# P x V of a causal attention on one core: column halves of the array given to the two heads of a pair, and the scaling done on the way out of PSUM

## The reference, cut to what matters

```python
B, S, D = x.shape                      # 2, 1024, 1024 ; H = 32 heads
q = (_rmsnorm(x @ wq_a.T, q_a_ln_w) @ wq_b.T).reshape(B, S, H, QHD)
...
scores = jnp.einsum('bqhd,bkhd->bhqk', q_full, k_full) * softmax_scale
scores = jnp.where(causal[None, None], scores, jnp.finfo(scores.dtype).min)
attn = jax.nn.softmax(scores, axis=-1)
out = jnp.einsum('bhqk,bkhd->bqhd', attn, v).reshape(B, S, H * VD)
return out @ wo.T
```

## Time and profile before

| | us |
|---|---|
| runs of the kernel | 1892.49 median, 1891.0 to 1895.84 (3 runs) |
| span of the profiled execution | 1895.1 |
| PE busy in it | 1803.7 (95%) |
| DVE, ACT, POOL busy | 1231.4 (65%), 1000.5 (53%), 877.8 (46%) |
| one pass of the loop (two steps) | 60.5, 14 times |

### The profile page before, as it was taken

One profiled execution on the slowest core, in us unless ns is written; L12 is line 12 of the kernel. 1 busy time (PEld: TensorE's weight loads), 2 busy tenths in 40 slices (PEclk: granted clock), 3 DMA queues, 4 the chain that ended last, 5 costly groups with the idle time before them and its releaser, 6 DMA issues. The chain is left out here.

```text
span 1895.1 us, 44298 instructions
## 1 busy us (share of the span) xinstructions
PE 1803.7 (95%) x15472; PEld 1422.9 (75%) x15472; DVE 1231.4 (65%) x2654; ACT 1000.5 (53%) x2137; POOL 877.8 (46%) x641
## 2 busy tenths in 40 slices
PE   5999969899999999999999999998999999989999
PEld 4788869877777777777777777775788888877887
DVE  5655358688898888889888888989521111125453
ACT  2221047788887888888787888877310100112110
POOL 3232112377777878777787878775000000014321
PEclk9999979999999999999999999999999999989999
DMA  6542162311212112121222212123742233224321
GB/s 217 193 156 100 67 173 94 84 62 44 86 59 78 57 62 80 57 80 40 85 69 68 69 51 82 55 86 113 249 151 89 94 100 115 67 87 158 130 89 59
DMA packets 111969, 182.74 MB, mean 96 GB/s; under 512 B 27680, under 2 KB 64672, under 8 KB 109856
## 3 DMA queue, kind: packets, MB, share of 16 engines
q1 hardware_dynamic: 111904, 181.88, 29.8%
HBM read 122.33 MB, written 59.51 MB: 96 GB/s over the span
## 5 line engine op out<-in xcount | busy, mean ns | idle before, releaser
L1290 PE MATMUL psS<-keyT,q 128*128 128x512 f32 (+2 forms) x2304 | 473.2, 350 | 23.9 <-POOL q L648 14.5
L1290 PEld LDWEIGHTS psS<-keyT,q 128*128 128x128 f32 x2304 | 381.2, 189 | 118.2 <-DVE negmax L1408 41.7
L1357 ACT ACTIVATE prob<-prob,negmax 128x640 f32<-128x640 f32 (+7 forms) x512 | 392.0, 767 | 78.5 <-DVE negmax L1408 75.9
L1418 DVE STREAM_TRANSPOSE pT<-prob 128x640 f32<-128x640 f32 (+7 forms) x512 | 379.9, 762 | 66.4 <-PE psV L1307 61.6
L1408 DVE CUSTOM_DVE_ANT_0 prob<-psS,mask 128x640 f32<-128x640 f32 (+7 forms) x512 | 371.9, 742 | 20.9 <-PE psS L1290 7.4
L469 PE MATMUL f_psy<-f_weff,f_xT 128*128 128x512 f32 x1344 | 315.6, 393 | 0.0
L1101 PE MATMUL psS<-o_w,o_o 128*128 128x512 f32 x1344 | 304.8, 389 | 0.0
L469 PEld LDWEIGHTS f_psy<-f_weff,f_xT 128*128 128x128 f32 x1344 | 250.9, 188 | 55.8
L1101 PEld LDWEIGHTS psS<-o_w,o_o 128*128 128x128 f32 x1344 | 252.3, 188 | 52.4
L1307 PE MATMUL psV<-pT,val 32*64 32x512 f32 (+3 forms) x8192 | 264.8, 407 | 6.4 <-DVE pT L1418 6.2
L1307 PEld LDWEIGHTS psV<-pT,val 32*64 32x64 f32 x8192 | 168.8, 132 | 109.7 <-issue 66.2
(11 more groups left out here) (120 smaller groups left out, 1919.1 us busy)
## 6 DMA issues: line engine op xcount, KB each, us to landing
wo<-in_wo SPq DMA_DIRECT2D x16, 1024.0 KB, 6.0
pT<-row_scales SPq DMA_DIRECT2D x128, 128.0 KB, 2.9
oT<-pT SPq DMA_DIRECT2D x64, 256.0 KB, 2.5
o_in<-oT SPq DMA_DIRECT2D x32, 512.0 KB, 5.2
f_xt<-in_x SPq DMA_DIRECT2D x16, 512.0 KB, 4.4
f_w_in<-in_w SPq DMA_DIRECT2D x16, 512.0 KB, 6.7
w_sum<-f_w_in SPq DMA_DIRECT2D x16, 512.0 KB, 5.3
x<-f_xo SPq DMA_DIRECT2D x16, 512.0 KB, 3.0
```

What stands on the lines that cost most here:

```text
L1290: ins = nc.tensor.matmul(psS[:, slot, start + x0:start + x1], q[:, e, a, t * P:(t + 1) * P], k.keyT[:, m, b * S + x0:b * S + x1], start=(i ...
L1357: nc.scalar.activation(row, row, ACT.Exp, bias=negmax[:, n % 8:n % 8 + 1], scale=-1.0, accum_out=rowsum[:, column(n, s):column(n, s) + 1]) ...
L1418: nc.vector.transpose(pT[:, n % 2, t, 0:width], prob[:, n % RING, 0:width]).then_inc(turned, 1)
```

## The change

V: the loops are now over the four key blocks (`block`), then the head (`e`), then the rows (`i`). Column half `e` takes head `e`, so a bank's partitions 0 to 63 are head 0 and 64 to 127 head 1, each with all key blocks summed. A matmul streams one head's columns, 32 x (8 - kt): 256 down to 32, and there are 32 of them for each kt. O: one DVE instruction a bank multiplies the bank of PSUM by `o_scale` into `o_raw` (four a step), behind waits on `valued` and, for bank 0, on both halves of `o_scale` and on the stores of the step before. ACT's copy, DVE's additions and POOL's multiplication are gone, `copied` and `evicted` too; `vacated` waits on `scaled`. In the last round ACT's preparation of output weights, which stood inside job O, stands behind all jobs. The order tables are new.

```diff
-POOL_STEP = ("B2+0 B3+0 A0+1 A1+1 B0+1 B1+1 P0-1 P1-1 A2+1 A3+1")
+POOL_STEP = ("B2+0 B3+0 A0+1 A1+1 B0+1 B1+1 A2+1 A3+1")
...
-                        sp.wait_ge(scaled, step * 2 + ch - 1)
+                        sp.wait_ge(scaled, step * 4)
...
-                sp.wait_ge(scaled, (it * 2 + s) * 2 + ch + 1)
+                sp.wait_ge(scaled, (it * 2 + s) * 4 + 4)
...
-                        pe.wait_ge(evicted, (it * 2 + s) * 4 + bank + 1)
+                        pe.wait_ge(scaled, (it * 2 + s) * 4 + bank + 1)
...
-                for a in range(BLOCKS // 2):
-                    for half in range(2):
+                for block in range(BLOCKS):
+                    for e in range(2):
                         for i in range(BLOCKS):
-                            rows, block = slice(32 * i, 32 * i + 32), BLOCKS // 2 * half + a
-                            x = kt * P + 32 * block
-                            out = psV[KVR * half:KVR * half + KVR, i, :].rearrange("p (e t r) -> p e t r", e=2, r=32)
-                            ins = nc.tensor.matmul(out[:, :, kt:QT, :], val[rows, b, block, kt, :], pT[rows, :, kt:QT, x:x + 32],
-                                                   start=(kt == 0 and a == 0), stop=(kt == QT - 1 and a == BLOCKS // 2 - 1))
+                            rows, x = slice(32 * i, 32 * i + 32), kt * P + 32 * block
+                            out = of_block(psV[KVR * e:KVR * e + KVR, i, :])
+                            ins = nc.tensor.matmul(out[:, kt:QT, :], val[rows, b, block, kt, :], pT[rows, e, kt:QT, x:x + 32],
+                                                   start=(kt == 0 and block == 0), stop=(kt == QT - 1 and block == BLOCKS - 1))
...
-            def evict_values(it, bank, s):
-
-                step = it * 2 + s
-                act.wait_ge(valued, step * QT + QT)
-                if later(step, 1):
-                    act.wait_ge(evicted, step * 4 + bank - 3)
-                nc.scalar.activation(upper(bank), psV[KVR:P, bank, :], ACT.Copy).then_inc(copied, 1)
...
-                dve.wait_ge(copied, step * 4 + bank + 1)
-                if later(step, 1):
+                if bank == 0:
+                    dve.wait_ge(valued, step * QT + QT)
                     for ch in range(2):
-                        dve.wait_ge(o_stored[ch], step * 16)
-                for e in range(2):
-                    x = slice(e * 32 * QT, (e + 1) * 32 * QT)
-                    halves = [y.rearrange("p (h t r) -> p h t r", h=2, r=32) for y in (psV[0:KVR, bank, x], upper(bank)[:, x])]
-                    ins = nc.vector.tensor_tensor(by_block(o_raw, bank)[KVR * e:KVR * e + KVR], halves[0], halves[1], ALU.add)
-                ins.then_inc(evicted, 1)
+                        dve.wait_ge(r_loaded[ch], step * 32 + 32)
+                        if later(step, 1):
+                            dve.wait_ge(o_stored[ch], step * 16)
+                values = of_block(psV[:, bank, :]).rearrange("p (h t) r -> p h t r", h=2)
+                nc.vector.tensor_tensor(by_block(o_raw, bank), values, by_block(o_scale, bank), ALU.mult).then_inc(scaled, 1)
...
-            def scale_values(it, ch, s):
-
-                step = it * 2 + s
-                pool.wait_ge(evicted, step * 4 + 4)
-                pool.wait_ge(r_loaded[ch], step * 32 + 32)
-                nc.gpsimd.tensor_tensor(o_raw[:, ch, :], o_raw[:, ch, :], o_scale[:, ch, :], ALU.mult).then_inc(scaled, 1)
```

More of the change, by code:

```diff
@@ L894 @@
 BLOCKS = P // 32
-PE_STEP = ("S8-1 F0-1 S9-1 F1-1 Q0+0 S10-1 S11-1 Q1+0 S12-1 S13-1 W0-1 S14-1 S15-1 Q2+0 Q3+0 S0+0 S1+0 S2+0 S3+0 S4+0 "
+PE_STEP = ("S8-1 F0-1 F1-1 S9-1 Q0+0 S10-1 S11-1 Q1+0 S12-1 S13-1 S14-1 W0-1 S15-1 Q2+0 Q3+0 S0+0 S1+0 S2+0 S3+0 S4+0 "
            "S5+0 S6+0 S7+0 V0-1 V1-1 V2-1 V3-1 V4-1 V5-1 V6-1 V7-1")
[L897 to L900, removed]
+ACT_STEP = ("F0-1 F1-1 E8-1 Q0+0 E9-1 E10-1 Q1+0 E11-1 E12-1 E13-1 H0+0 W0-1 E14-1 H1+0 Q2+0 E15-1 Q3+0 H2+0 E0+0 E1+0 "
+            "E2+0 E3+0 E4+0 E5+0 E6+0 E7+0 H3+0")
+DVE_STEP = ("T12-1 T13-1 M15-1 T14-1 M0+0 M1+0 M2+0 M3+0 T15-1 R1-1 T0+0 T1+0 M4+0 M5+0 M6+0 T2+0 M7+0 T3+0 T4+0 T5+0 "
+            "T6+0 T7+0 O0-1 O1-1 M8+0 F0+0 R0+0 M9+0 O2-1 O3-1 T8+0 F1+0 M10+0 M11+0 T9+0 T10+0 M12+0 M13+0 T11+0 "
             "M14+0")
-POOL_STEP = ("B2+0 B3+0 A0+1 A1+1 B0+1 B1+1 P0-1 P1-1 A2+1 A3+1")
+POOL_STEP = ("B2+0 B3+0 A0+1 A1+1 B0+1 B1+1 A2+1 A3+1")
 SP_STEP = ("X1-1 Y0-1 Y1-1 K0+0 L0+0 X0+0 Z0+0")
@@ L1134, in attention_phase @@
         r_stored, r_loaded = c.sem("r_stored"), [c.sem(f"r_loaded{ch}") for ch in range(2)]
-        valued, copied, evicted, scaled = c.sem("valued"), c.sem("copied"), c.sem("evicted"), c.sem("scaled")
+        valued, scaled = c.sem("valued"), c.sem("scaled")
         o_stored = [c.sem(f"o_stored{ch}") for ch in range(2)]
@@ L1169, in folds, with of_block @@
             return 2 * (it + (s + 1) // 2) + n + 1
-        def upper(bank):
-            return (cosT, sinT)[bank // 2][0:KVR, bank % 2 * BANK:(bank % 2 + 1) * BANK]
+        def of_block(bank):
+            return bank[:, 0:32 * QT].rearrange("p (t r) -> p t r", r=32)
         def by_block(tile, i):
@@ L1383, in body @@
                         copy_output_weights(r.it, s)
-                    elif job == "O":
-                        if r.last and s == 1 and n == 0:
-                            act.wait_ge(scored, TILES * units)
-                            output.weights_hi(nc, act, range(SLOTS))
-                            act.wait_ge(turned, TILES * units)
-                            output.weights_hi(nc, act, range(SLOTS, 2 * SLOTS))
-                        evict_values(r.it, n, s)
                     elif job == "F":
@@ L1393, in _ @@
             rounds(act, body)
+            act.wait_ge(scored, TILES * units)
+            output.weights_hi(nc, act, range(SLOTS))
+            act.wait_ge(turned, TILES * units)
+            output.weights_hi(nc, act, range(SLOTS, 2 * SLOTS))
+            act.wait_ge(valued, QT * units)
             output.weights_hi(nc, act, range(2 * SLOTS, 14))
@@ L1459, in body @@
                             output.weights_lo(nc, dve, range(2 * SLOTS))
-                        join_values(r.it, n, s)
+                        scale_values(r.it, n, s)
                     elif job == "F":
@@ L1474, in query_lo @@
                 queries.low(nc, pool, qf[:, n % 2, :], n, (it * 2 + s) * 4 + n)
[L1476 to L1481 removed]
             def finished(it, job, n, s):
[L1484 to L1487 removed]
+                pool.wait_ge(queries.roped if job == "A" else q_lo, (it * 2 + s) * 4 + n + 1)
             def body(r):
@@ L1499, in body @@
                         query_lo(r.it, n, s)
-                    elif job == "P":
-                        scale_values(r.it, n, s)
             rounds(pool, body)
```

6 lines of the change are left out of this document (1 added, 5 removed).

## The result

The changed kernel takes **2140.9 us** (median of 4 runs, 2135.3 to 2142.4), the kernel before 1893.6 us beside it on the same chip: a ratio of 1.130, 95% interval 1.128 to 1.132. The prediction was 2118 us, 84% for slower. The profiled execution spans 2140.6 us for 1895.1, +245.5.

A forecast was written before the change was run, and what follows sets the result against it. TensorE was taken as the bound, VectorE close behind. The span of 1895.1 us + 205 (products) + 53 (branch back) - 32 (waits) made 2121, as a median 2118 us; range 1905 to 2210, likeliest case 2043 to 2197.

The forecast's parts named there:

- 26 products: P x V products in the attention loop: each waits for its code, +6.4 us on 8.2; all 32 products +205 us.
- branch back: TensorE's loop branch, 13 taken: goes to code no longer in the store, one full fetch each, 4.1 us, +53 us.
- waits: TensorE's waits for VectorE's maxima and GpSimd's q in the loop: -1.0 us a step, -32 us, bounds 0 and -45.
- The size of the store: TensorE's instruction store holds a pass of 6 packets but not 10, so each pass fetches its code again; chance 0.57.
- a store that holds the larger loop: Rival for TensorE's loop: only six products in new code pay; about 1938 us (1915 to 1965); 0.26 with the VectorE-bound rival.
- 2.3 + 3 x 4.1 = 14.6 us: Time of a P x V product: 2.3 us uses up one packet of code, then three waits of 4.1 us each.
- a clock that falls as TensorE idles: Tail case, with fetches queuing behind data as its other reason: slower than 2220 us, chance 0.01.
- M12 behind two transposes: New order table: maximum M12 stands behind T9 and T10, two 1 us transposes, while scores wait; gives back part of the gain.
- The rival in which VectorE becomes the bound: Through M12 behind two transposes, TensorE's wait for maxima stays 1.2 us a step; 1965 us; 0.26 with the larger-loop rival.
- The stream: P x V columns: 64 narrow records need at least 0.84 us; kt 5, 6, 7 rise +0.19 +0.42 +0.42, about +1.0 us a step.
- the six products in new code: Four products outside the loop and two in its first pass fetch new code: 6 x 6.4 = 38 us.
- The likeliest case: TensorE's loop code is fetched again in each pass: 2118 us, own range 2043 to 2197, chance 0.57.

The follow-up runs named there:

- The three split kernels: Kernel before, each P x V matmul cut in two by head for all eight kt, kt 0 to 2, or kt 0 to 3: 2224.7, 2087.2 and 2107.7 us.
- the kernel before with all pieces split: Kernel before with every P x V matmul, all eight kt, written as two, one for each head; tables and way out as before: 2224.7 us, ratio 1.175.

## Why the prediction was right, point by point

The mechanism was the forecast one, code fetched again in each pass. The total is closer than the terms are: two errors of opposite sign nearly cancel, and that part is luck. The account of the 13 passes, 216.0 us, beside the prediction's terms for the same 13 passes:

| term | predicted | measured | from |
|---|---|---|---|
| 26 products | 26 x 6.4 = +166 | 26 x 4.54 = +118 | first to last matmul start 12.53 us, before 7.99 |
| branch back | 13 x 4.1 = +53 | 13 x 4.24 = +55 | its median, 4454 less 215 ns |
| waits | -26 | -28 | changed kernel with wide matmuls, 58.4 for 60.5 a pass |
| clock | 0 | up to +62 | an estimate from the half-clock time, below |
| rest | 0 | about +9 | TensorE's issue gaps of up to 0.7 us at F0 and Q0 |

The products and the branch are read from the changed kernel itself; the waits are carried over from another kernel and the clock is an upper estimate, so that the sum closes doesn't check each of them.

- **The size of the store: right.** 9.9 packets' worth don't stay. The three split kernels show it with nothing else changed. The 0.26 for a store that holds the larger loop was generous: it does not hold 7.4.
- **The branch back: right**, 4.24 us for 4.1 each. The changed kernel written straight, without branch, is 55 us faster, with products that are 0.6 us longer.
- **The products: right in kind, too large.** The step that was mis-sized is "2.3 + 3 x 4.1 = 14.6 us". Packets inside a product came 3.7 us apart on average (3.3 to 4.9), not 4.1; that makes 2.3 + 3 x 3.7 = 13.4. And a product doesn't wait three times: its first packet falls 1.4 us behind its start on average, what is already there carries it that far, and the list of waits has 59 waits in 26 products, 2.3 each. 12.5 us were measured, +4.5 for +6.4, 48 us less than forecast in the 13 passes and close to the low bound of +4.3. That bound came from the packets of the earlier trace rows, 3.4 us apart; the loop's pace lies between them and the 4.1.
- **The clock: the term that was put at nothing.** The prediction names "a clock that falls as TensorE idles" only in the tail of 0.01. It falls in every pass. A granted clock of 0.91 over 1003 us is 180 us at the lower level; less the 13 gaps of about 4.3 us that lie in it, some 124 us of work ran at half speed, which costs at most 62. The two errors have opposite signs, and the total came out 23 us short.
- **The waits: right**, -1.07 us a step for -1.0. Of the part on the tables, the fear that M12 behind two transposes gives part back weighed little: 13.3 us of waits for maxima are left of 31.6 in the kernel with the wide matmuls. The rival in which VectorE becomes the bound falls.
- **The stream: too high**, +0.5 for +0.84 at kt 6 and 7. In the changed kernel it can't be told from the fetches: of the 4.5 us that a product grew, 3.0 are idle time (78.6 us in 26 products), and the other 1.5 are the slower stream and its restarts together.
- Outside the 13 passes lie 29.5 us: the six products in new code, for which the prediction had 38 less 6 of waits.

The likeliest case was the one that came, and its own range, 2043 to 2197, holds the time. That range is not all terms at their ends, as the prediction says: it keeps the waits at -32. With their ends, 0 and -45, it is about 2030 to 2226. What stays open: why the kernel before with all pieces split is 84 us slower than the change. In the 13 passes it is 76 us. 56 of them are products of 14.7 us for 12.5 at the same number of instructions; the rest is of the size of what the tables and the way out were worth, up to 28. Its packets came 4.0 us apart in place of 3.7, which makes less than half of the 2.2 us. The clock makes another part: it reads 0.88 over these passes for 0.91, and lower inside products too, as in this one, where 128 matmuls took 3.10 us for the 1.91 of the changed kernel (801.9 to 805.3 us):

```profile
801.90:805.30 3.40, 3.10 (x128) 2.91 (x128) 0.00 (x0) 0.00 (x0) 1.06 (x1) 0.50 0.22 81
```

Why its packets come later and its clock is lower, no run tells.

## What to carry to other kernels

Count the instructions of an engine's loop, not only its work: a change that trades adds on idle engines for more, narrower TensorE instructions may push the loop out of the instruction store, and the branch and every dense stretch then pay. In the profile it shows as packets on the instruction queue inside a loop that had none, "issue" gaps on an engine that waits for nobody, and a branch of 4 us. When TensorE is made to idle in small pieces, add the clock to the bill: here it cost up to as much as the branch. And an order table belongs to its division of work: with another, the same table cost 65 us where it had been part of a gain.

## What the runs showed of the hardware

- A TensorE loop of 6.4 packets' worth of code (1630 instructions) stayed in its store; at 6.9 the passes took turns (once two that fetched in a row), one without a packet, the next with nine; at 7.4 every pass fetched. A pass that fetched brought about two packets more than its code fills: 9 for 6.9, 12 for the 9.9 of the changed kernel.
- Packets for which a product of the changed kernel waited came 3.3 to 4.9 us apart, 3.7 on average, and TensorE went on 1.2 to 1.6 us after each had been moved; at one packet's worth in 4.1 us the fetch was all but hidden (1.0005).
- The granted clock fell to 1.2 GHz behind a product with gaps of only 1.2 and 1.8 us in it, and stayed there for some 7 us of unbroken work (757.4 to 765.0 us of the changed kernel written straight).
- 64 matmuls of 32 x 64 arrays with 32 or 64 columns took about 0.7 us, 10 to 11 ns each; 32 with twice the columns 0.42.
